# A graph network on one core: GpSimd takes part of the one-hot work in the building of the adjacency matrix, and a small load changes its queue

## The chip, the cores and the metric

The kernel runs as one launch on one core of a Trainium2 chip. The metric is device time in microseconds of that core, as the median of several runs. One further execution was recorded by the hardware profiler; its trace is where every row below comes from. The engines are TensorE (PE, with PEld for its weight loads), VectorE (DVE), ScalarE (ACT), GpSimd (POOL) and SyncE (SP); a q behind a name (ACTq, SPq) marks what the engine's instruction queue does by itself, such as register work and the issuing of DMAs.

## The reference, cut to what matters

Four graph layers follow one another on 3125 nodes and 50000 edges: a three-layer graph convolution, an attention layer, a gated edge layer, and a ten-layer deep graph convolution with norms. The change touches only what comes before the first of them. A graph convolution is

```
deg = segment_sum(w, d)                     # the edges into each node, and its self loop
dinv = where(deg > 0, rsqrt(deg), 0)
norm = dinv[s] * w * dinv[d]
out = segment_sum(h[s] * norm[:, None], d)  # + bias
```

The kernel does the sum over edges as a dense product: it first builds the matrix A of 3125 x 3125 with A[source, target] = sum of the weights w of the edges between them (self loops with weight 1), stores it in DRAM, and the layers read it from there. `dinv` is multiplied in outside of A.

## The kernel before

**What `build_adjacency` does.** The edges come sorted by target. Six target nodes make a group; a group's edges are in `lane_words`, one edge on each of the 128 partitions (122 edges and the 6 self loops), with four words: the row of the source within its tile of 125 nodes, the place of source tile and target, the weight, and the tile. For each group a one-hot of the source row (`ohr`, 128 edges x 125, compared with a ramp) and a weighted one-hot of the place (`cell`, 128 edges x 150) are multiplied on TensorE, which gives the group's six columns of A. Row 125 of the one-hots is all ones, so that the same product gives the degrees.

**Units and blocks.** Three groups make a unit (index `n`, 174 of them), about 25 units make a block of 450 columns (index `b`, seven blocks, `j` is the unit within its block; block 4 has 24 units). For each unit:

- VectorE makes `ohr` (L495, one instruction for the three groups) unless `n % 3 == 1`, and always makes `cell` (L499). Once in four units it makes the factors of the cells (L469, L477, L480).
- ScalarE makes `ohr` for the units with `n % 3 == 1` (`byact`), in four instructions (L587 three times, L590 once), four units ahead (`EARLY`).
- TensorE does the three products (L555; each is recorded as two passes, so a unit has six MATMUL records) into one of five PSUM banks (`BANKS`).
- ScalarE copies the sums from PSUM to the block's columns `stage` (L609).

`ohr` and `cell` are rings of five units (`RING`), so VectorE may be five units ahead of TensorE; five banks let TensorE be five units ahead of ScalarE's copies.

**Extra edges.** A few groups have more than 122 edges. What is left over comes in extra blocks of edges (index `i`; with these inputs eight in all, one for each block of columns and two for block 5). They are handled in loops whose bounds are read from memory by every engine that takes part: SyncE loads the 122 edges' words and the first cell (L631, L632), GpSimd makes their one-hot and cells (L434, L435, L437), TensorE multiplies (L539), ScalarE copies the sum (L598), VectorE adds it to the columns (L453). The extras of block `b - 1` are in TensorE's and ScalarE's program behind unit `j == EXTRA_AT` (2) of block `b`, and in VectorE's behind unit `j == EXTRA_AT + RING` (7). Only when VectorE has added them does SyncE store the block's degree row (L635) and its 5.6 MB of columns (L636).

**Order.** Each engine runs its own program in order; semaphores tie them: `s_oh` counts VectorE's units, `s_ao` ScalarE's one-hots, `s_mm` TensorE's units, `s_ev` ScalarE's copies, `s_om` the words' DMAs (32 for one extra), `s_oo` GpSimd's extras, `s_omm` TensorE's, `s_oc` ScalarE's, `s_od` VectorE's, `s_blk` the finished blocks. After the last block come the degrees, their square root, and the first layer.

## Time and profile before

| | us |
|---|---|
| median of 3 runs (lowest, highest) | 3285.01 (3284.21, 3285.78) |
| the profiled execution's own time | 3285.47 |
| its span, from the first to the last instruction | 3283.5 |
| the stretch from the first product of a unit (L555) to the last extra's addition (L453) | 35.4 to 228.0 |
| TensorE, VectorE, ScalarE, GpSimd busy in the whole span | 3106.7, 1370.8, 1408.2, 846.8 |

The stretch that the change touches is some 6% of the span. Busy time over the whole span says little of it: TensorE's 3106.7 us are mostly the layers behind it. The rows that follow are therefore taken from inside the stretch. "Idle before" in square brackets is how long the engine stood still just before an instruction, and who let it go on.

### The profile page before, as it was taken

The page shows a single profiled execution, that of the slowest core. Times are in us where ns is not written, and L with a number is a line of the kernel's source. Part 1 is how long each engine was busy: PE and PEld are TensorE (multiplying, and loading weights), DVE is VectorE, ACT ScalarE, POOL GpSimd, SP SyncE. Part 2 cuts the span into 40 slices and gives each one's busy share as a digit, 9 for nine tenths or more (in the row PEclk, how much of TensorE's full clock was granted, in tenths as well). Part 3 has the DMA queues.
Part 4 walks back from the last instruction along what each step waited for, and adds up shares of the span by engine and source line. Part 5 has one row for each costly group of instructions (what it writes and reads, how often), then busy time and mean ns, then how long its engine had stood idle before and what let it go on. Part 6 is the DMA issues. An engine that isn't in the chain of part 4 may idle for free. (4 is left out here: it accounts for less than half of the span.)

```text
span 3283.5 us, 45208 instructions
## 1 busy us (share of the span) xinstructions
PE 3106.7 (95%) x14568; PEld 2006.1 (61%) x14568; DVE 1370.8 (42%) x3096; ACT 1408.2 (43%) x2506; POOL 846.8 (26%) x939
## 2 busy tenths in 40 slices
PE   7879999979999998999999799999999999999998
PEld 6865555547788775777777555555555555555554
DVE  7971110125666667999999511111111111111112
ACT  6860000225555555888888423333332222222333
POOL 2010000037777763777777000000000000000000
PEclk8989999989999998999999899999999999999999
DMA  2556667723333323666666467666677766777774
GB/s 90 231 236 243 273 282 286 286 61 83 87 83 83 83 70 92 186 194 184 186 185 183 181 288 288 283 284 281 284 287 290 290 281 281 290 291 298 290 298 169
DMA packets 166699, 709.29 MB, mean 216 GB/s; under 512 B 39287, under 2 KB 133090, under 8 KB 153423
## 3 DMA queue, kind: packets, MB, share of 16 engines
q1 hardware_dynamic: 127865, 618.84, 48.5%
q0 software_dynamic: 33600, 83.09, 9.1%
q10 hardware_dynamic: 5011, 4.48, 0.5%
q8 instruction: 129, 2.11, 0.3%
q14 instruction: 94, 0.77, 0.1%
HBM read 657.91 MB, written 48.07 MB: 215 GB/s over the span
## 5 line engine op out<-in xcount | busy, mean ns | idle before, releaser
L1422 PE MATMUL deep_out_psum<-deep_adjacency,deep_scaled_nodes_odd 125*128 125x450 f32 (+1 forms) x1750 | 669.7, 537 | 0.0
L1422 PE MATMUL deep_out_psum<-deep_adjacency,deep_scaled_nodes 125*128 125x450 f32 (+1 forms) x1750 | 669.7, 537 | 0.0
L1670 POOL DMA_INDIRECT source_rows<-gat_source_rows,pair_src x416 | 396.5, 953 | 575.3 <-POOLq L64 448.8
L1422 PEld LDWEIGHTS deep_out_psum<-deep_adjacency,deep_scaled_nodes_odd 125*128 125x128 f32 x1750 | 328.4, 189 | 299.8 <-issue 298.9
L1422 PEld LDWEIGHTS deep_out_psum<-deep_adjacency,deep_scaled_nodes 125*128 125x128 f32 x1750 | 328.1, 189 | 298.9 <-issue 298.0
L2100 POOL DMA_INDIRECT near_room<-gate_source_rows,pair_src x416 | 395.1, 950 | 141.7 <-issue 119.2
L1480 ACT ACTIVATE deep_squares_high<-deep_aggregate,deep_vectors 128x450 fp32r<-128x450 f32 (+1 forms) x70 | 46.7, 668 | 618.1 <-DVE deep_aggregate L1552 618.1
L1422 PE MATMUL gcn_out_psum<-adjacency_columns,gcn_scaled_nodes 125*128 125x450 f32 (+1 forms) x700 | 268.7, 538 | 0.0
L2198 PE MATMUL gate_banks<-edge_weights,edge_features_t 128*128 128x256 f32 x832 | 248.4, 380 | 0.0
L1566 DVE SCALAR_TENSOR_TENSOR deep_normed<-deep_aggregate,deep_vectors,deep_squares 128x450 f32<-128x450 f32 (+1 forms) x70 | 47.9, 684 | 384.9 <-ACT deep_squares L1489 384.9
L1422 PEld LDWEIGHTS gcn_out_psum<-adjacency_columns,gcn_scaled_nodes 125*128 125x128 f32 x700 | 131.2, 190 | 123.5 <-issue 122.8
L2200 PE MATMUL gate_banks<-gate_target_rows,gate_node_onehot_t 125*128 x1248 | 204.7, 271 | 0.0
L1552 DVE TENSOR_TENSOR deep_aggregate<-deep_out_psum,dinv_all 128x450 f32<-128x450 f32 (+1 forms) x70 | 43.6, 624 | 348.7 <-PE deep_out_psum L1422 348.7
L1487 ACT ACTIVATE deep_squares<-deep_moments,deep_eps 128x450 f32<-128x450 f32 (+1 forms) x70 | 44.4, 634 | 330.0 <-PE deep_moments L1393 330.0
L1824 ACT ACTIVATE score_terms_sloped<-score_terms_psum 128x512 f32<-128x512 f32 x104 | 62.1, 597 | 250.6 <-PE score_terms_psum L1714 245.4
L555 PE MATMUL adjacency_sum<-h_t,dinv_all 128*128 128x150 f32 x1042 | 155.8, 305 | 13.3 <-DVE h_t L499 12.4
L2209 PE MATMUL gate_banks<-gate_node_onehot,gate_messages 128*128 128x125 f32 x832 | 122.0, 290 | 45.6 <-DVE gate_messages L2390 45.6
L1287 POOL TENSOR_TENSOR identity_branch<-identity_branch,x_t 128x450 f32<-128x450 f32 (+1 forms) x7 | 7.9, 1128 | 600.8 <-ACT identity_branch L1271 600.8
L2200 PEld LDWEIGHTS gate_banks<-gate_target_rows,gate_node_onehot_t 125*128 125x128 bf16 x1248 | 120.9, 97 | 66.5
L555 PEld LDWEIGHTS adjacency_sum<-h_t,dinv_all 128*128 128x128 f32 x1042 | 142.7, 196 | 25.8 <-DVE h_t L499 22.3
L1714 PE MATMUL score_terms_psum<-att_node_onehot_t,near_room 125*128 125x128 bf16 x1248 | 155.2, 226 | 0.2
L1712 PE MATMUL score_terms_psum<-ident,source_rows 128*128 128x128 f32 x416 | 119.2, 286 | 33.8 <-issue 23.0
(418 smaller groups left out, 4754.0 us busy)
## 6 DMA issues: line engine op xcount, KB each, us to landing
deep_adjacency<-adjacency SPq DMA_DIRECT2D x69, 5625.0 KB, 16.2
adjacency_columns<-adjacency SPq DMA_DIRECT2D x19, 5625.0 KB, 16.1
adjacency<-adjacency_columns SPq DMA_DIRECT2D x7, 5625.0 KB, 17.7
edge_features<-in_edge_attr_dram SPq DMA_DIRECT2D x416, 64.0 KB
att_node_rows<-pair_dst_rows SPq DMA_DIRECT2D x104, 128.0 KB
gate_node_rows<-pair_dst_rows SPq DMA_DIRECT2D x104, 128.0 KB, 3.3
source_rows<-gat_source_rows,pair_src POOLq DMA_INDIRECT x416, 2.5
near_room<-gate_source_rows,pair_src POOLq DMA_INDIRECT x416
```

The costliest lines, as they stand in the source:

```text
L555: i = nc.tensor.matmul(acc[:, n % BANKS, q * CELLS:(q + 1) * CELLS], ohr[:, n % RING, q, :], cell[:, n % RING, q, :], start=True, stop=True)
L1422: m = nc.tensor.matmul(op[:, n % 2, 0:cols], h[l % 2][:, s, :], ring[0:T, n % 2, s, 0:cols], start=s == 0, stop=s == NS - 1)
L1480: nc.scalar.activation(sq_high[:, 0:cols], yk, ACT.Square, bias=row[0])
L1566: vec.scalar_tensor_tensor(yb[:, 0:cols], yk, vecs[:, l:l + 1], sq[:, 0:cols], ALU.add, ALU.mult).then_inc(s_nm, 1)
L1670: pool.indirect_dma_start(xj[:, b % HOLD, q, :], None, d["h_r"], bass.IndirectOffsetOnAxis(ap=c["pair_src"][:, b * PQ + q:b * PQ + q + 1], ...
L1712: nc.tensor.matmul(o, xj[:, b % HOLD, q, :], c["ident"][:, :], start=True, stop=False, is_transpose=True)
L1714: m = nc.tensor.matmul(o, rows[:, p, bass.ds(tile[q], 1), :].rearrange("r o f -> r (o f)"), oht[:, b % 2, q * 128:(q + 1) * 128], start=Fa ...
L1824: nc.scalar.activation(low[:, b % 2, :], p_z[:, b % 2, :], ACT.Copy, scale=SLOPE).then_inc(s_lo, 1)
L2100: pool.indirect_dma_start(xj[:, b % 4, q, :], None, d["p_src"], bass.IndirectOffsetOnAxis(ap=c["pair_src"][:, b * PQ + q:b * PQ + q + 1], ...
L2198: nc.tensor.matmul(o, e_t[:, b % 2, q * 128:(q + 1) * 128], we[:, :], start=True, stop=False)
L2200: m = nc.tensor.matmul(o, oht[:, b % 2, q * 128:(q + 1) * 128], rows[:, p, bass.ds(tile[q], 1), :].rearrange("r o f -> r (o f)"), start=Fa ...
L2209: m = nc.tensor.matmul(p_a[:, q * T:(q + 1) * T], msg[:, b % 2, q, :], oh[:, b % 4, q, :], start=True, stop=True)
```

## The change

It does four things, all inside `build_adjacency`.

1. GpSimd makes `ohr` for the units of `bypool`: `n % 3 == 0` and `j >= POOL_FROM` (9), in block 0 only up to `n` = 21. That is five units in each block and six in block 3, 36 in all. It takes three instructions of 128 x 125 for a unit (107 in all, since one unit has two groups). VectorE leaves out L495 for them, and TensorE waits for `s_po` as well.
2. GpSimd makes the one-hot and cells of extra `i + 1` in the loop turn of extra `i`, after TensorE has used those of `i`; those of extra 0 are made by code ahead of the loop of block 0.
3. The words of an extra are loaded by ScalarE, on its own DMA queue: those of extra 0 behind unit `n == LISTED_AT` (21), those of extra `i + 1` behind the copy of the sum of extra `i`. SyncE's loop goes away. One more extra than exists is loaded at the end, and ScalarE waits for it.
4. The lower and upper bound that the engines read may be at most `UO - 1`.

```diff
         CHUNK = 4
         SPREAD_AT, PLACED_AT, FIRST_AT, LISTED_AT, DEGREE_AT = 6, 13, 14, 21, 16
         EARLY = 4
+        POOL_FROM = EXTRA_AT + RING + 2
         tab = c["lane_words"]
         ohr = c["dinv_b"][:, 0:RING * SUB * 128].rearrange("p (k q r) -> p k q r", k=RING, q=SUB)
         cell = c["h_t"][:, 0:RING * SUB * CELLS].rearrange("p (k q i) -> p k q i", k=RING, q=SUB)
...
         names = ("onehots_initialised", "onehots_ready", "sums_ready", "sums_read", "extra_loaded", "extra_onehots_ready", "extra_summed", "extra_read",
                  "extra_done", "columns_done", "extra_local", "degrees_copied", "extras_spread", "extras_placed", "extras_listed", "extra_step",
                  "distances_ready", "far_onehots_ready", "sixes_ready", "members_marked", "marks_ready", "degrees_summed", "degree_step", "degree_guarded", "degree_root", "dinv_ready", "dinv_turned",
-                 "dinv_copied")
+                 "dinv_copied", "pool_onehots_ready")
         (s_p, s_oh, s_mm, s_ev, s_om, s_oo, s_omm, s_oc, s_od, s_blk, s_loc, s_dg, s_xs, s_xp, s_xl, s_xv,
-         s_af, s_ao, s_t6, s_mb, s_mk, s_d, s_v, s_in, s_rt, s_n, s_t, s_c) = (c["sems"].take("build_" + n) for n in names)
+         s_af, s_ao, s_t6, s_mb, s_mk, s_d, s_v, s_in, s_rt, s_n, s_t, s_c, s_po) = (c["sems"].take("build_" + n) for n in names)
         s_st = c["adj_stored"]
         units = [(b, j, u) for b in range(NSP) for j, u in enumerate(UNITS[b])]
         ends = [sum(len(UNITS[k]) for k in range(b + 1)) for b in range(NSP)]
         slot = [(b + NSP - HELD) % 2 for b in range(NSP)]
         byact = [n for n in range(len(units)) if n % 3 == 1]
+        bypool = [n for n, (b, j, u) in enumerate(units) if n % 3 == 0 and j >= POOL_FROM and (b > 0 or n < LISTED_AT + 3)]
         block = ctx.enter_context(nc.Block())
 
         def bounds(eng, b):
             if b == 0:
                 eng.wait_ge(s_xl, 1)
-            return [eng.value_load(c["extra_bounds"][0:1, b + k:b + k + 1], min_val=k, max_val=UO) for k in range(2)]
+            return [eng.value_load(c["extra_bounds"][0:1, b + k:b + k + 1], min_val=k, max_val=UO - 1) for k in range(2)]
 
         @block.gpsimd
         def _(pool):
...
             pool.wait_ge(s_p, 2)
             pool.sem_inc(s_oo, 1)
             for b in range(NSP):
+                for n in (n for n in bypool if units[n][0] == b):
+                    u, k = units[n][2], n % RING
+                    g0, m = u[0], len(u)
+                    if n >= RING:
+                        pool.wait_ge(s_mm, n - RING + 1)
+                    for q in range(m):
+                        i = g.tensor_scalar(ohr[:, k, q, 0:T], c["ramp"][:, 0:T], tab[:, 0, g0 + q:g0 + q + 1], None, ALU.is_equal)
+                    i.then_inc(s_po, 1)
+                if b == 0:
+                    pool.wait_ge(s_om, 32)
+                    g.tensor_tensor(local[:, :], more[:, 1:2], first_cell[:, :], ALU.subtract).then_inc(s_loc, 1)
+                    g.tensor_scalar(xohr[:, 0:T], c["ramp"][:, 0:T], more[:, 0:1], None, ALU.is_equal)
+                    pool.wait_ge(s_loc, 1)
+                    g.tensor_scalar(xcell[:, :], c["ramp"][:, 0:CELLS], local[:, 0:1], more[:, 2:3], ALU.is_equal, ALU.mult).then_inc(s_oo, 1)
                 lo, hi = bounds(pool, b)
                 with pool.Fori(lo, hi) as i:
-                    wait_alone(pool, c, s_om, (i + 1) * 32)
-                    wait_alone(pool, c, s_omm, i + 1)
+                    wait_alone(pool, c, s_om, (i + 2) * 32)
+                    wait_alone(pool, c, s_omm, i + 2)
                     g.tensor_tensor(local[:, :], more[:, 1:2], first_cell[:, :], ALU.subtract).then_inc(s_loc, 1)
                     g.tensor_scalar(xohr[:, 0:T], c["ramp"][:, 0:T], more[:, 0:1], None, ALU.is_equal)
-                    wait_alone(pool, c, s_loc, i + 1)
+                    wait_alone(pool, c, s_loc, i + 2)
                     g.tensor_scalar(xcell[:, :], c["ramp"][:, 0:CELLS], local[:, 0:1], more[:, 2:3], ALU.is_equal, ALU.mult).then_inc(s_oo, 1)
 
         @block.vector
...
                     members_of(h + 1)
                 if n % CHUNK == 2:
                     marks_of(h + 1)
-                if n not in byact:
+                if n not in byact and n not in bypool:
                     vec.tensor_tensor(ohr[:, k, 0:m, 0:T], c["ramp"][:, 0:T].unsqueeze(1).to_broadcast([128, m, T]),
                                       tab[:, 0, g0:g0 + m].unsqueeze(2).to_broadcast([128, m, T]), ALU.is_equal)
                 dve.wait_ge(s_mk, h + 1)
...
                 pe.wait_ge(s_oh, n + 1)
                 if n in byact:
                     pe.wait_ge(s_ao, byact.index(n) + 1)
+                if n in bypool:
+                    pe.wait_ge(s_po, bypool.index(n) + 1)
                 if n >= BANKS:
                     pe.wait_ge(s_ev, n - BANKS + 1)
                 for q in range(len(u)):
...
                     wait_alone(act, c, s_omm, i + 2)
                     wait_alone(act, c, s_od, i + 1)
                     nc.scalar.copy(xsum[:, :], xacc[:, 0:CELLS]).then_inc(s_oc, 1)
+                    e0 = act.value_load(c["extra_first"][0:1, bass.ds(i + 1, 1)], min_val=0, max_val=E)
+                    act.dma_start(more[0:EL, :], d["edges"][bass.ds(e0, EL), :]).then_inc(s_om, 16)
+                    act.dma_start(first_cell[:, :], c["extra_cells"][:, bass.ds(i + 1, 1)]).then_inc(s_om, 16)
+                return hi
 
             for n in range(EARLY):
                 if n in byact:
...
                                acc[:, n % BANKS, 0:m * CELLS].rearrange("p (q s j) -> p s q j", q=m, j=G)).then_inc(s_ev, 1)
                 if n + EARLY in byact:
                     onehots(n + EARLY)
+                if n == LISTED_AT:
+                    act.wait_ge(s_p, 2)
+                    act.wait_ge(s_xl, 1)
+                    e0 = act.value_load(c["extra_first"][0:1, 0:1], min_val=0, max_val=E)
+                    act.dma_start(more[0:EL, :], d["edges"][bass.ds(e0, EL), :]).then_inc(s_om, 16)
+                    act.dma_start(first_cell[:, :], c["extra_cells"][:, 0:1]).then_inc(s_om, 16)
                 if b >= 1 and j == EXTRA_AT:
                     extras(b - 1)
-            extras(NSP - 1)
+            extra = extras(NSP - 1)
+            wait_alone(act, c, s_om, (extra + 1) * 32)
             act.wait_ge(s_in, 1)
             nc.scalar.activation(root, safe, ACT.Sqrt).then_inc(s_rt, 1)
             act.wait_ge(s_t, 1)
...
         def _(sp):
             ly.begin(sp, d)
             for b in range(NSP):
-                lo, hi = bounds(sp, b)
-                with sp.Fori(lo, hi) as i:
-                    e0 = sp.value_load(c["extra_first"][0:1, bass.ds(i, 1)], min_val=0, max_val=E)
-                    wait_alone(sp, c, s_oo, i + 1)
-                    sp.dma_start(more[0:EL, :], d["edges"][bass.ds(e0, EL), :]).then_inc(s_om, 16)
-                    sp.dma_start(first_cell[:, :], c["extra_cells"][:, bass.ds(i, 1)]).then_inc(s_om, 16)
                 sp.wait_ge(s_blk, b + 1)
                 first = ORDER[b] * BW
                 sp.dma_start(c["degree_parts"][0:NS, first:first + BW], stage[T:T + 1, slot[b], :, :]).then_inc(s_dg, 16)
```

What stands where, on three engines. Line numbers of the changed kernel differ (before/changed: L609/L631 the copy of a unit's sums, L598/L616 the copy of an extra's, L587 and L590/L605 and L608 ScalarE's one-hots, L416/L418 the bounds, L434, L435, L437/L450, L451, L453 an extra on GpSimd).

ScalarE's queue before, from the one-hots of unit 28 through the extra of block 0 to the next unit's copies:

```order
L587 ACTIVATE dinv_all<-ramp,lane_words 128x125 x3
L590 ACTIVATE dinv_all<-dinv_all 128x3x125
L416 TENSOR_LOAD extra_bounds
L416 ISA x2
L416 TENSOR_LOAD extra_bounds
L416 ISA x2
L595 UNCONDITIONAL_BRANCH
L595 ISA
L31 REGISTER_ALU
L598 COPY extra_sum<-extra_adjacency_sum 128x150
L595 REGISTER_ALU
L595 COMPARE_AND_BRANCH
```

and the same place in the changed kernel, from the extra's copy on:

```order
L616 COPY extra_sum<-extra_adjacency_sum 128x150
L617 ISA
L617 TENSOR_LOAD extra_first
L617 ISA x2
L618 ISA
L618 DMA extra_words<-edge_list 122x4
L619 REGISTER_ALU
L619 DMA extra_first_cell<-extra_cells 128x1
L613 REGISTER_ALU
L613 COMPARE_AND_BRANCH
L631 COPY adjacency_columns<-adjacency_sum 128x25x18 x3
```

A register load, its checks and two DMA issues now stand between the extra's copy and the copies of the following units.

GpSimd's queue in the changed kernel, blocks 0 and 1 (before, only the rows of the loops, with L434, L435 and L437, stand here):

```order
L438 TENSOR_SCALAR dinv_all<-ramp,lane_words 128x125 x15
L442 TENSOR_TENSOR extra_cell<-extra_words,extra_first_cell 128x1
L443 TENSOR_SCALAR extra_source_onehot<-ramp,extra_words 128x125
L445 TENSOR_SCALAR extra_weighted_cell<-ramp,extra_cell,extra_words 128x150
L418 TENSOR_LOAD extra_bounds
L447 ISA
L450 TENSOR_TENSOR extra_cell<-extra_words,extra_first_cell 128x1
L451 TENSOR_SCALAR extra_source_onehot<-ramp,extra_words 128x125
L453 TENSOR_SCALAR extra_weighted_cell<-ramp,extra_cell,extra_words 128x150
L438 TENSOR_SCALAR dinv_all<-ramp,lane_words 128x125 x15
```

The one-hots of block 1 stand behind the loop that makes extra 1, so they wait for that extra's words too. SyncE's queue before, for block 0:

```order
L629 TENSOR_LOAD extra_first
L629 ISA x2
L31 REGISTER_ALU
L631 ISA
L631 DMA extra_words<-edge_list 122x4
L632 REGISTER_ALU
L632 DMA extra_first_cell<-extra_cells 128x1
L635 DMA degree_parts<-adjacency_columns 25x1x450
L636 DMA adjacency<-adjacency_columns 128x11250
```

Of these only the last two stay on SyncE.

## Rows read from the trace of the kernel before

**Rows 1.** The page: its head.
```profile
span 3283.5 us, 45208 instructions
```

**Rows 2.** Windows between ScalarE's copies of extras: busy us (count), clock, DMA.
```profile
core 0: us, PE busy (x) PEld busy (x) DVE busy (x) ACT busy (x) POOL busy (x), PEclk, DMA share, GB/s
...
97.43:123.15 25.72, 22.42 (x156) 20.16 (x155) 24.91 (x61) 22.92 (x58) 2.39 (x3) 1.00 0.56 228
...
151.41:175.94 24.53, 22.74 (x157) 21.14 (x156) 24.11 (x60) 21.99 (x58) 1.64 (x3) 0.96 0.59 238
...
200.79:204.87 4.08, 1.10 (x4) 1.13 (x5) 1.92 (x5) 0.29 (x1) 2.28 (x3) 0.54 0.00 0
```

**Rows 3.** Waits from 69.6 to 226 us: total us, times, longest.
```profile
ACT adjacency_columns L609 <- PE adjacency_sum L555: 11.2, 27, 1.0
...
PE extra_adjacency_sum L539 <- POOL extra_weighted_cell L437: 5.9, 3, 4.0
```

**Rows 4.** Timeline of ScalarE, units 19 to 24 and the first extra: start, duration.
```profile
62.76 1.39 ACT L609 COPY adjacency_columns<-adjacency_sum 128x450 f32<-128x450 f32 x3
...
65.05 0.52 ACT L590 ACTIVATE dinv_all<-dinv_all 128x375 f32<-128x375 f32 x1
65.47 1.39 ACT L609 COPY adjacency_columns<-adjacency_sum 128x450 f32<-128x450 f32 x3
...
72.18 0.28 ACT L598 COPY extra_sum<-extra_adjacency_sum 128x150 f32<-128x150 f32 x1 [1.18 <-issue]
```

**Rows 5.** Timeline, VectorE: a one-hot and the cells behind it.
```profile
62.28 0.53 DVE L495 TENSOR_TENSOR dinv_all<-ramp,lane_words 128x375 f32<-128x375 f32 x1
62.73 0.60 DVE L499 TENSOR_TENSOR h_t<-h_t,group_member_psum 128x450 f32<-128x450 f32 x1
```

**Rows 6.** SyncE's load of one extra's words: the register load, the issues, GpSimd's start.
```profile
L629 SPq TENSOR_LOAD <-extra_first x8: 282/978/1169, 62.9 to 209.5; - x8
...
63.75 0.30 SPq L631 DMA_DIRECT2D extra_words<-edge_list  x1
64.16 0.59 SPq L632 DMA_DIRECT2D extra_first_cell<-extra_cells  x1
...
66.20 0.83 POOL L434 TENSOR_TENSOR extra_cell<-extra_words,extra_first_cell 128x1 f32<-128x1 f32 x1 [32.29 <-DMA extra_first_cell<-extra_cells]
```

**Rows 7.** GpSimd's instructions, alone and beside VectorE's.
```profile
L435 POOL TENSOR_SCALAR extra_source_onehot<-ramp,extra_words x8: 610/615/1091, 67.0 to 224.8; 128x125 f32<-128x125 f32 x8
...
67.64 1.61 POOL L437 TENSOR_SCALAR extra_weighted_cell<-ramp,extra_cell,extra_words 128x150 f32<-128x150 f32 x1
67.97 0.22 DVE L469 TENSOR_TENSOR group_member_psum<-ramp,lane_words 128x72 f32<-128x72 f32 x1
68.12 0.53 DVE L495 TENSOR_TENSOR dinv_all<-ramp,lane_words 128x375 f32<-128x375 f32 x1
...
146.01 0.88 POOL L437 TENSOR_SCALAR extra_weighted_cell<-ramp,extra_cell,extra_words 128x150 f32<-128x150 f32 x1
146.16 0.71 DVE L495 TENSOR_TENSOR dinv_all<-ramp,lane_words 128x375 f32<-128x375 f32 x1
```

**Rows 8.** Timeline at the first and second extra on TensorE, and GpSimd's last.
```profile
69.65 0.49 PE L539 MATMUL extra_adjacency_sum<-extra_weighted_cell,extra_source_onehot 128*128 128x150 f32 x2 [1.05 <-POOL extra_weighted_cell L437]
70.05 4.07 PE L555 MATMUL adjacency_sum<-h_t,dinv_all 128*128 128x150 f32 x30
...
201.10 0.19 POOL L434 TENSOR_TENSOR extra_cell<-extra_words,extra_first_cell 128x1 f32<-128x1 f32 x1 [2.57 <-DMA extra_first_cell<-extra_cells]
203.77 0.84 PE L539 MATMUL extra_adjacency_sum<-extra_weighted_cell,extra_source_onehot 128*128 128x150 f32 x2 [3.96 <-POOL extra_weighted_cell L437]
...
224.63 0.19 POOL L434 TENSOR_TENSOR extra_cell<-extra_words,extra_first_cell 128x1 f32<-128x1 f32 x1 [21.25 <-DMA extra_first_cell<-extra_cells]
...
227.41 0.28 ACT L598 COPY extra_sum<-extra_adjacency_sum 128x150 f32<-128x150 f32 x1 [1.80 <-PE extra_adjacency_sum L539]
```

**Rows 9.** A window of 2 us behind TensorE's 4 us stop (columns as in Rows 2).
```profile
204.00:206.00 2.00, 2.00 (x9) 2.00 (x10) 0.32 (x1) 0.28 (x1) 0.00 (x0) 0.50 0.00 0
```

## The prediction

> **What bounds the kernel now.** The span is 3283.5 us [rows 1], and the profiled execution took 3285.47 us, 0.46 above the median; what moves inside the span moves the time one for one, because TensorE goes straight on into the first layer when the stretch is over. I read the windows between ScalarE's copies of two extras first, since in order of program one such copy stands in each block and 25 units lie between two of them. In [rows 2] the 25.72 us window has VectorE busy for 24.91: it is the bound there. But ScalarE has 22.92, and in the 24.53 us window it is hardly behind. Then I looked for how fast ScalarE could go at all. In [rows 4] it works without a pause: the copies of units 19 to 21 start at 62.76, those of 22 to 24 at 65.47, so three units with one set of one-hots take 2.71 us, 0.90 a unit, 22.6 for 25. To this comes the reading of the bounds ahead of an extra (idle 1.18 at 72.18 [rows 4]) and the extra's copy; part of the reading can lie beside the engine's last instruction, so I take 1.0 for both. ScalarE alone would need 23.6 us for a block. VectorE needs for three units two one-hots, three cells and three quarters of the factors: its slot for a one-hot is 0.45 us (62.28 to 62.73 [rows 5]). TensorE does five units in 4.07 us [rows 8], 0.81 a unit, and is not the bound. So VectorE bounds most blocks, with ScalarE 2 us behind it. From 69.6 to 226 us ScalarE waited 11.2 us for TensorE's sums [rows 3]; that is all the room the change can open before ScalarE is the bound.
>
> **One-hots to GpSimd.** 36 one-hots leave VectorE: 36 x 0.45 = 16.2 us. Two or three of block 0 (n = 9, 12, 15) fall where VectorE waits for TensorE's ten extra products anyway. Were VectorE the only limit, about 15 us would go. It is not: the room is 11.2 us.
>
> GpSimd's price for one: three instructions like L435, at 0.61 us [rows 7], 1.8 us; its units come every three, some 2.7 us apart, so it keeps up if nothing holds it. What could hold it shows in [rows 7]: the cells of an extra took 0.88 us in one place and 1.61 in another, where VectorE's L469 (0.22) and L495 (0.53) ran at the same time; the difference, 0.73, is their sum. At 146.16 it was VectorE that was held: 0.71 for an instruction of 0.53. The Trainium skill (SBUF — State Buffer, "Who interferes with whom") says that a VectorE instruction with two SBUF inputs contends with a GpSimd instruction that reads SBUF, and that one of them blocks. L495 and L469 read two SBUF tensors, and the trace agrees by the 0.73. I take 1.8 to 2.9 us a unit: the high end is 1.8 and all of VectorE's such instructions in three units, one L495 (0.53) and three quarters of the factors (about 0.5). The 4 units of lead that the ring gives, 3.3 us or more, cover either.
>
> **The words on ScalarE's queue.** This is the cost. On SyncE the register load begins at 62.9, the first issue at 63.75, and the second ends at 64.16 + 0.59 = 64.75: 1.85 us [rows 6]. On ScalarE this train stands behind the extra's copy, and the next copy, which came 0.2 us after the extra's, cannot be dispatched before it is through: 1.75 us more for each. The cheapest reading is the two issues alone, 0.30 + 0.50 = 0.8; the dearest has the register load at SyncE's median of 0.98 and a blocked issue, near 3. I take 1.75, since nothing else is on this queue and the store of the block comes after. Seven such trains lie ahead of the last extra's copy, 12.25 us; the one behind unit 21 begins while L590 (65.05) still runs and holds the copies from 65.47, 1.4 us, at a place where ScalarE has no room [rows 4]. Sum 13.65 us. The train behind the last copy, and ScalarE's wait for it, lie beside the last degree row's way to TensorE through VectorE and SyncE, and cost nothing; without that cover they would cost 1.85.
> The Trainium skill (DMA: Bandwidth & Descriptors, "Issuing engines are not separate DMA queues") holds that all queues run on the same 16 DMA engines and another issuer saves only sequencer time. By that rule the move gives the transfer nothing and only shifts the 1.85 us from an idle engine to a busy one.
>
> **Extras one block early.** Before, the words of the last extra came at 224.63, and ScalarE's last extra copy waited 1.80 us; it would have been through the bounds 1.1 us sooner than 227.41 [rows 8]. That 1.1 is won. TensorE's other waits for GpSimd (5.9 us in three [rows 3]) are mostly the second extra of block 5, which does not get better. Now its words are issued only behind the first one's copy: 1.85 for the train, 1.45 until GpSimd starts (64.75 to 66.20 [rows 6]), 2.67 until TensorE starts (201.10 to 203.77) and 1.10 until ScalarE's copy, 7.1 us in place of 4.08 [rows 2, 8]. That is 3.0 longer, of which 1.75 is counted: 1.25 more.
>
> **What is late next.** GpSimd makes extra i + 1 before the one-hots of its block. From TensorE's product of an extra (0) ScalarE's copy comes at about 2.5 (69.65 to 72.18), the train ends at 4.4, GpSimd starts at 5.8, is through at 8 and has its first unit at 10.2. TensorE wants unit j = 9 at about 8.2 (the one-hots of j = 7 come from ScalarE at 6.4, behind the train, then 0.9 a unit). So it is 2 us late in blocks 3 and 6, whose first unit is j = 9, one in blocks 2 and 5 (j = 10), nothing in 1 and 4 (j = 11). ScalarE has two copies in hand then and loses about half: 2.1 us in all, taken from its room.
>
> **Sum.** + 13.65 (trains) + 1.25 (second extra) + 2.1 (late first units) - 11.2 (ScalarE's waits for sums) - 1.1 (last words) = + 4.7 us. 3285.0 + 4.7 = 3289.7 us. A measurement of this kernel tells some 0.2% (6.6 us) from no change, so I expect none that counts: 0.50 for within 6.6 us by this mechanism.
>
> **Rivals.**
> *ScalarE's train is cheap, and VectorE's relief shows* (0.20, faster). If the train costs the two issues alone, 0.8 each, and partly lies where ScalarE waits, the trains come to 6.4 less some 3 and the sum is - 5 to - 8; at no price at all it is VectorE's 15 us less 2 for the rest, 3272. I put 3277. For it: in the 25.72 us window ScalarE had 2.8 us free. Against: the 24.53 us window is within 0.9 of ScalarE's own need. It decides at a train under 0.9 us.
> *GpSimd is the bound* (0.20, slower). If each reading instruction is fully blocked by VectorE's, a unit takes 2.9 us where the cycle is 2.7, and what starts 2 us late stays late to the block's end. Six blocks at 2 to 3 us: + 15, less nothing, since ScalarE is the bound behind it; with the sum of the other terms 3285 + 2.6 + 12 = 3300. For it: the 1.61 us [rows 7]. Against: most L435 ran in 0.61 beside a busy VectorE. It decides at 2.7 us a unit.
> *TensorE's clock* (0.10, slower). Behind its stop of 3.96 us it was granted 0.50 of full speed, the 1.2 GHz level, and did 9 matmuls in 2 us [rows 8, 9]. If every block's new stop did that, each would cost 1 to 1.5 us of the slack: + 7, with the sum 3296.
>
> **Range and chances.** The bounds of the train move the sum by 8 x 0.95 down and 8 x 1.2 up, GpSimd's by 12 up. 8 in 10 lies in 3277 to 3301; the likeliest case alone in 3284 to 3296. Faster by more than 6.6 us 0.18, within 0.50, slower 0.32: the forecast's own upper edge adds to the slower rivals.
>
> **What the changed trace would show.** ScalarE: behind each extra's copy 1.7 to 1.9 us without work, its waits for sums under 3 us. VectorE: idle for 10 us or more that it had not been. GpSimd: units at 1.8 to 2.3 us. TensorE: waits for GpSimd's one-hots in blocks 3 and 6, hardly in 1 and 4; the second extra of block 5 some 7 us behind the first. The last sum of a unit no earlier than 225. I am wrong if ScalarE still waits 8 us or more for sums, or if its gap behind an extra is under 1 us.

## The result, and the profile after

| | before | changed |
|---|---|---|
| median of 4 runs each (lowest, highest), us | 3285.40 (3284.21, 3286.71) | 3309.68 (3308.34, 3310.02) |
| span of the profiled execution, us | 3283.5 | 3308.0 |
| from the first product of a unit to the last extra's addition, us | 35.4 to 228.0 = 192.6 | 36.6 to 253.5 = 216.9 |

The ratio is 1.0073, with a 95% interval from 1.0061 to 1.0085: slower by 24.3 us. The forecast was 3289.7 with a range of 3277 to 3301; the result is 20.0 above the one and 8.7 above the upper edge of the other. The stretch alone is longer by 216.9 - 192.6 = 24.3 us, so the whole loss lies in it. From here on "the stretch" is this length.

The windows between ScalarE's copies of extras, after, in the last four blocks (columns as in [rows 2]):

```profile
125.20:153.16 27.96, 24.28 (x179) 22.88 (x178) 24.26 (x58) 23.90 (x63) 13.60 (x21) 1.00 0.51 209
153.16:179.31 26.15, 22.48 (x154) 21.43 (x153) 22.54 (x54) 22.03 (x57) 10.60 (x17) 0.93 0.55 224
179.31:214.45 35.14, 23.51 (x134) 21.65 (x132) 23.80 (x56) 22.80 (x58) 10.53 (x18) 0.76 0.41 166
214.45:220.89 6.44, 1.11 (x4) 1.14 (x5) 0.32 (x1) 0.28 (x1) 1.64 (x3) 0.63 0.02 0
220.89:252.93 32.04, 21.07 (x139) 20.14 (x138) 15.41 (x36) 18.64 (x47) 10.45 (x18) 0.81 0.44 182
```

The first is as long as its block before (28.3), the second 1.6 us longer (24.5 before). The third and the fifth are some 10 us too long, every engine is idle for some 11 us or more in them, and the granted clock fell to 0.76 and 0.81. The fourth is the second extra of block 5, 6.44 in place of the 4.08 of [rows 2]. So the loss is not a tax on each block; two places hold most of it. The waits from 69.6 to 252 us (columns as in [rows 3]):

```profile
POOL extra_cell L450 <- DMA extra_first_cell<-extra_cells: 88.6, 7, 20.5
ACT adjacency_columns L631 <- PE adjacency_sum L573: 28.9, 16, 9.9
...
PE adjacency_sum L573 <- issue: 18.1, 10, 9.7
...
POOL dinv_all L438 <- PE adjacency_sum L573: 17.0, 19, 1.8
...
PE extra_adjacency_sum L555 <- POOL extra_weighted_cell L453: 6.6, 1, 6.6
```

ScalarE now waits 28.9 us for sums where it waited 11.2 [rows 3], the longest 9.9 and not 1.0. TensorE's own longest wait is 9.7 us, "issue": the profile names no releaser. The timeline of all engines there, in block 5 (start, duration, idle before in brackets; SyncE's and ScalarE's DMA issues are the rows with SPq and ACTq), says who it was:

```profile
180.10 0.48 ACTq L618 DMA_DIRECT2D extra_words<-edge_list  x1
180.68 0.51 ACTq L619 DMA_DIRECT2D extra_first_cell<-extra_cells  x1
181.24 0.45 SPq L659 DMA_DIRECT2D adjacency<-adjacency_columns  x1
...
187.65 0.54 ACT L631 COPY adjacency_columns<-adjacency_sum 128x450 f32<-128x450 f32 x1 [0.34 <-PE adjacency_sum L573]
...
190.48 0.19 POOL L450 TENSOR_TENSOR extra_cell<-extra_words,extra_first_cell 128x1 f32<-128x1 f32 x1 [20.46 <-DMA extra_first_cell<-extra_cells]
...
192.09 3.49 POOL L438 TENSOR_SCALAR dinv_all<-ramp,lane_words 128x125 f32<-128x125 f32 x6
193.96 1.34 PE L573 MATMUL adjacency_sum<-h_t,dinv_all 128*128 128x150 f32 x4 [6.34 <-issue]
```

The words of the next extra are issued, done at 181.19; 0.05 us later SyncE begins to issue the block's store (called 5.6 MB above; it is 128 rows of 11250 numbers, 45 KB each, 5.76 MB in all). GpSimd can start on the words only at 190.48, 9.3 us after their issue, against the 1.45 of [rows 6]. GpSimd's first one-hots of the block (L438) stand behind the loop that waits for those words, so they come at 192.09, and TensorE starts again at 193.96, 1.87 us later, when three of these six instructions (3.49 / 2 = 1.75 us) are through. The DMA view shows what the words met (queue, kind: packets, MB, share of the 16 engines' time; q1 carries SyncE's DMAs, q10 ScalarE's). In block 5, from 180 to 184 us, from 184 to 190, and of that from 186 to 190:

```profile
q1 hardware_dynamic: 34, 0.58, 45.9%
q10 hardware_dynamic: 232, 0.00, 3.0%
...
q1 hardware_dynamic: 71, 2.84, 111.4%
q10 hardware_dynamic: 36, 0.00, 0.3%
...
q10 hardware_dynamic: 7, 0.00, 0.1%
```

The two loads are 268 small packets of 16 or 4 bytes. In block 4 all 268 were on their way by 155.95 us, before the first packet of q1. In block 5 only 232 were by 184; the other 36 come one by one or a few together between the store's packets, seven of them behind 186, and none behind 190. From 184 to 190 q1 has 63 packets of 45 KB, which took some 1.7 us each (111.4% of 16 engines and 6 us, over 63). So the late packets of the words wait for turns of the store that last 1.7 us each, and the last of them for several.

### The profile page after: what moved, and what is told of

Same layout as the page of the kernel before. It is cut to its first block and busy times, and to the rows that moved or that the text cites. A ratio compares the mean times of both kernels' runs of the same rounds, so it can differ in the third digit from the quotient of the medians.

```text
span 3308.0 us, 45234 instructions
## 1 busy us (share of the span) xinstructions
PE 3110.3 (94%) x14568; PEld 2016.7 (61%) x14568; DVE 1355.1 (41%) x3060; ACT 1407.6 (43%) x2507; POOL 917.1 (28%) x1049
## 5 line engine op out<-in xcount | busy, mean ns | idle before, releaser
L573 PE MATMUL adjacency_sum<-h_t,dinv_all 128*128 128x150 f32 x1042 | 156.7, 310 | 34.9 <-issue 18.4
L1575 DVE TENSOR_TENSOR deep_aggregate<-deep_out_psum,dinv_all 128x450 f32<-128x450 f32 (+1 forms) x70 | 43.6, 623 | 348.7 <-PE deep_out_psum L1445 348.7
L573 PEld LDWEIGHTS adjacency_sum<-h_t,dinv_all 128*128 128x128 f32 x1042 | 148.6, 204 | 42.3 <-issue 21.9
## 6 DMA issues: line engine op xcount, KB each, us to landing
deep_adjacency<-adjacency SPq DMA_DIRECT2D x69, 5625.0 KB, 16.2
adjacency_columns<-adjacency SPq DMA_DIRECT2D x19, 5625.0 KB, 16.2
adjacency<-adjacency_columns SPq DMA_DIRECT2D x7, 5625.0 KB, 17.7
```

The source lines that it names most:

```text
L573: i = nc.tensor.matmul(acc[:, n % BANKS, q * CELLS:(q + 1) * CELLS], ohr[:, n % RING, q, :], cell[:, n % RING, q, :], start=True, stop=True)
```

## The race, block by block

Issue of the words' second DMA (start plus duration), the store's issue, and GpSimd's start, in the changed kernel; the last column is the time from the words' issue to GpSimd's start on them:

| block | words' issue ends | store's issue starts, ends | GpSimd starts | words' issue to GpSimd |
|---|---|---|---|---|
| 1 | 76.96 | 77.19, 78.66 | 79.04 | 2.08 |
| 2 | 102.53 | 102.62, 103.31 | 103.97 | 1.44 |
| 3 | 127.05 | 127.90, 128.35 | 128.50 | 1.45 |
| 4 | 155.02 | 155.10, 155.79 | 156.46 | 1.44 |
| 5 | 181.19 | 181.24, 181.69 | 190.48 | 9.29 |
| 6 | 222.92 | 222.82, 223.27 | 233.62 | 10.70 |

Where the store's issue ends 0.77 us or more behind the words' the load takes 1.4 to 2.1 us; where it ends 0.50 or 0.35 behind, 9 to 11. The words have to be through before SyncE's packets come: in block 4 they were, in block 5 they were not, as the DMA view shows. Block 6's is the second stop:

```profile
237.10 7.01 PE L573 MATMUL adjacency_sum<-h_t,dinv_all 128*128 128x150 f32 x42 [9.75 <-issue]
```

The Trainium skill (DMA: Bandwidth & Descriptors, "Queues, rings and completion order") says that a DMA engine serves its queues in turn and changes only between packets. By that rule a small load on another queue should be late beside a large store, yet not by the whole of it. The trace agrees: the words' packets went on between the store's, seven of them behind 186 us, and were through after some 9 us, where the store took 17.3 us from its issue to its landing. How the packets were spread over the 16 engines the trace does not tell.

## The experiments

The chips of these runs granted TensorE less clock in later stages of the network (kernel before: medians of 3805.89 for e1 to e4, 3712.97 for e5 to e8, 3708.51 for e9 and e10), and the totals scatter by more than the effects. From 600 to 1200 us of the span, for one, the clock was 0.96 before and 0.78 in e9. In the stretch and up to 600 us it was 1.00 but for low spans of 3 to 20 us behind pauses of TensorE, so the stretch is what I compare. Three kernels ran twice, and their stretches differed by 1.8, 1.3 and 0.2 us; before's 192.6 is from one profile. Starts and ends are rounded to 0.1 us, and so is what is said below.

The time from one ScalarE copy of an extra to the next (first column: first product of a unit to the first such copy), made of the starts of those instructions in each trace:

| kernel | to the first | b1 | b2 | b3 | b4 | b5 | second extra | b6 | stretch |
|---|---|---|---|---|---|---|---|---|---|
| before | 36.8 | 25.3 | 25.7 | 28.3 | 24.5 | 24.9 | 4.1 | 22.5 | 192.6 |
| changed | 38.5 | 25.6 | 24.5 | 28.0 | 26.2 | 35.1 | 6.4 | 32.0 | 216.9 |
| e10 changed again | 38.3 | 25.6 | 24.5 | 30.0 | 25.7 | 34.3 | 6.4 | 33.3 | 218.7 |
| e1 store waits | 37.6 | 25.6 | 25.5 | 28.0 | 25.7 | 27.5 | 6.4 | 23.6 | 200.6 |
| e2 no GpSimd one-hots | 38.4 | 26.4 | 25.5 | 27.8 | 25.3 | 26.3 | 6.4 | 21.9 | 198.4 |
| e3 one-hots alone | 37.2 | 23.8 | 24.7 | 25.6 | 23.2 | 24.1 | 4.0 | 22.5 | 185.7 |
| e4 words by SyncE | 36.7 | 23.8 | 24.1 | 25.4 | 23.2 | 23.4 | 4.5 | 22.2 | 183.9 |
| e8 e4 again | 35.9 | 23.8 | 24.1 | 25.4 | 23.2 | 23.4 | 4.5 | 21.6 | 182.6 |
| e7 e4 with idle trains | 36.6 | 25.5 | 25.4 | 27.3 | 26.9 | 27.1 | 4.4 | 21.9 | 195.7 |
| e6 words a turn early | 37.1 | 23.7 | 24.1 | 25.1 | 23.3 | 23.5 | 2.5 | 21.5 | 181.6 |
| e9 e6 again | 35.9 | 23.7 | 24.1 | 25.1 | 23.3 | 23.5 | 2.8 | 22.3 | 181.4 |
| e5 words behind the store | 35.9 | 43.2 | 42.0 | 46.5 | 42.3 | 43.6 | 5.4 | 39.4 | 298.8 |

### e1: SyncE's store waits for the words

```diff
             for b in range(NSP):
+                lo, hi = bounds(sp, b)
                 sp.wait_ge(s_blk, b + 1)
...
+                wait_alone(sp, c, s_om, (hi + 1) * 32)
                 sp.dma_start(d["adj"][ORDER[b]], stage[:, slot[b], :, :]).then_inc(s_st[slot[b]], 16)
```

> The changed kernel, with one wait more: SyncE issues a block's 5.6 MB store only when the words of the next extra have landed. Theory A (the words lose a race with the store on the DMA engines, and GpSimd's one-hots are queued behind the words): the stops of TensorE of 6.3 and 9.8 us in blocks 5 and 6 go, with 3 us of low clock behind them; 3288 to 3294 us, words landing 1.5 to 2.5 us behind their issue in every block. Theory B (GpSimd's one-hots are slowed by VectorE's reads and bound the blocks): nothing changes, 3303 to 3312. Theory C (ScalarE's issue trains are the loss): 3303 to 3312 as well, since the trains stay.

The stretch was 34.4 to 235.0 = 200.6 us; total 3821.35 against 3805.89, ratio 1.0041 (1.0012 to 1.0070). In block 5 the store went a microsecond after the words, not at the same time:

```profile
178.20 0.51 ACTq L619 DMA_DIRECT2D extra_first_cell<-extra_cells  x1
...
179.97 0.33 SPq L661 DMA_DIRECT2D adjacency<-adjacency_columns  x1
...
180.16 0.19 POOL L450 TENSOR_TENSOR extra_cell<-extra_words,extra_first_cell 128x1 f32<-128x1 f32 x1 [12.64 <-DMA extra_first_cell<-extra_cells]
```

The words took 1.45 us again (in block 6 3.05, where only the block's degree row, 25 packets of 1.8 KB, was in their way). Both long stops are gone, and with them 216.9 - 200.6 = 16.3 of the 24.3 us: block 5 is shorter by 7.6 and block 6 by 8.4. Only the order of two transfers was changed: that is the race. 8.0 us stay.

### e2: no one-hots on GpSimd

```diff
-        bypool = [n for n, (b, j, u) in enumerate(units) if n % 3 == 0 and j >= POOL_FROM and (b > 0 or n < LISTED_AT + 3)]
+        bypool = []
```

> The changed kernel with an empty list of GpSimd's units: VectorE makes those one-hots again; the early extras and the words on ScalarE's queue stay. Theory A: late words hold nobody but the extra itself, which is needed 20 us later, so no stop of TensorE over 2 us but the second extra of block 5; VectorE bounds again and the trains take ScalarE's room: 3286 to 3297. Theory B: the same, so this run does not tell A from B. Theory C: 3300 or more, since the trains stay.

34.9 to 233.3 = 198.4 us; ratio 1.0023 (0.9989 to 1.0058). ScalarE's trains are all there, and the race is lost in the same two blocks: in block 5 the words' issue ends at 180.08 and GpSimd starts at 189.35, 9.3 us later; in block 6 it is 10.8. But no unit stands behind the words, and no stop before a unit's product is over 2.0 us. So the late words hurt by way of GpSimd's one-hots. Against e1 the one-hots are worth + 2.2 us, hardly more than the 1.8 by which two profiles of one kernel differed: with the trains on ScalarE, no gain of VectorE's relief is to be seen.

### e3: GpSimd's one-hots alone

The kernel before with the `bypool` lines of the diff for GpSimd, VectorE and TensorE, and nothing else.

> The kernel before with the 36 units' one-hots on GpSimd and nothing else of the change: SyncE loads the words, and an extra's one-hots are made in its own block, behind that block's unit one-hots. Theory A: no unit waits for words of the same moment; ScalarE becomes the bound without any train, 4 to 10 us faster than before, 3275 to 3282. Theory B: GpSimd's pace bounds here too, slower than before, 3295 or more. Theory C: 3275 to 3282.

36.0 to 221.7 = 185.7 us, - 6.9; ratio 1.0016 (0.9980 to 1.0053). The waits from 34 to 260 us:

```profile
POOL dinv_all L438 <- PE adjacency_sum L567: 63.1, 35, 8.7
...
ACT adjacency_columns L621 <- PE adjacency_sum L567: 15.4, 21, 3.1
PE extra_adjacency_sum L549 <- POOL extra_weighted_cell L447: 13.9, 8, 3.7
```

GpSimd waited 63.1 us for rings to come free: it was early, not the bound. What this version pays is TensorE's 13.9 us of waits for extras (7.5 before, in the same window), since GpSimd reaches them behind its own units.

### e4 and e8: the words by SyncE, ahead of the store

ScalarE's loads go away, and SyncE gets a loop in place of them:

```diff
+                lo, hi = bounds(sp, b)
+                with sp.Fori(lo, hi) as i:
+                    e0 = sp.value_load(c["extra_first"][0:1, bass.ds(i + 1, 1)], min_val=0, max_val=E)
+                    wait_alone(sp, c, s_omm, i + 2)
+                    sp.dma_start(more[0:EL, :], d["edges"][bass.ds(e0, EL), :]).then_inc(s_om, 16)
+                    sp.dma_start(first_cell[:, :], c["extra_cells"][:, bass.ds(i + 1, 1)]).then_inc(s_om, 16)
                 sp.wait_ge(s_blk, b + 1)
```

> The changed kernel, but SyncE issues the words of extra i + 1, as soon as TensorE has used extra i and ahead of the block's store in its own queue; ScalarE issues nothing in the loops. Theory A: no race and no trains, the words land before the store starts: 3276 to 3287. Theory B: 3300 or more. Theory C: 3276 to 3290, the time of the trains (12 us) off the one of e1_store_waits or more. e1_store_waits less this run is the price of the trains: 12 us if ScalarE is the bound all the way, 3 to 8 if it has room.

35.2 to 219.1 = 183.9 us, - 8.7; the interval of the total's ratio, 1.0005 to 1.0145, is wide and its centre (1.0075) on the other side of the medians (3797.43 against 3805.89), so the total says nothing. The same kernel once more, e8:

> The same kernel as e4_words_by_sync, beside the other three on one chip: stretch 183 to 185, and a time that can be set against theirs; where the chip grants TensorE its clock as it did for the changed kernel, 3274 to 3280 us.

34.5 to 217.1 = 182.6 us, - 10.0; ratio 0.9988 (0.9939 to 1.0038). The stretch is 0.4 under what I had expected. The first and second part of the change shorten the stretch when ScalarE's queue has no part in them: from e1 to e4 it is 16.7 us.

### e7: e4, and the trains on ScalarE with nothing behind them

```diff
                     nc.scalar.copy(xsum[:, :], xacc[:, 0:CELLS]).then_inc(s_oc, 1)
+                    e0 = act.value_load(c["extra_first"][0:1, bass.ds(i + 1, 1)], min_val=0, max_val=E)
+                    wait_alone(act, c, s_id, i * 32 + 1)
+                    act.dma_start(idle_words[0:EL, :], d["edges"][bass.ds(e0, EL), :]).then_inc(s_id, 16)
+                    act.dma_start(idle_cell[:, :], c["extra_cells"][:, bass.ds(i + 1, 1)]).then_inc(s_id, 16)
```

> e4_words_by_sync with ScalarE's trains put back without a use: behind each extra's copy ScalarE loads the register and issues the same two DMAs, into tiles that nobody reads; the real words still come by SyncE ahead of the store. Only the price of the trains is added. Theory A with my 1.75 us for each: 8 x 1.75 less what ScalarE had as room, stretch 183.9 + 5 to 14 = 189 to 198. Theory C (the trains are the whole loss of the change): 210 or more.

35.4 to 231.1 = 195.7 us: 11.8 over e4, 13.1 over e8; ratio 1.0014 (0.9970 to 1.0059). Block by block over e4 (from the unrounded starts): 1.66, 1.36, 1.89, 3.69, 3.66, then - 0.07 and - 0.26. Blocks 4 and 5 pay double. TensorE in e7, block 4:

```profile
153.09 1.84 PE L575 MATMUL adjacency_sum<-h_t,dinv_all 128*128 128x150 f32 x6 [2.15 <-ACT adjacency_columns L635]
```

and the windows around it, first e7, then e4 at the same place of the program (columns as in [rows 2]):

```profile
152.00:154.00 2.00, 0.92 (x4) 0.95 (x5) 2.00 (x7) 1.60 (x5) 1.12 (x2) 0.76 0.90 286
154.00:156.00 2.00, 1.59 (x7) 1.26 (x7) 2.00 (x6) 1.97 (x7) 0.00 (x0) 0.50 0.92 345
156.00:158.00 2.00, 2.00 (x10) 2.00 (x10) 1.78 (x5) 1.97 (x7) 0.73 (x1) 0.50 0.84 360
158.00:160.00 2.00, 2.00 (x10) 2.00 (x10) 0.98 (x2) 0.91 (x2) 1.29 (x3) 0.53 0.89 383
```

```profile
149.00:151.00 2.00, 1.45 (x11) 1.22 (x10) 2.00 (x5) 1.97 (x7) 1.46 (x3) 1.00 0.93 346
151.00:153.00 2.00, 2.00 (x18) 2.00 (x17) 2.00 (x7) 1.98 (x6) 0.63 (x2) 1.00 0.84 360
```

While ScalarE issues, no copy frees a bank; TensorE stops for 2.15 us, and behind the stop it is granted 0.50, the 1.2 GHz level, for some 7 us: 10 matmuls in 2 us in place of 18. Then ScalarE, in the 158 window busy for 0.91 us, waits for it. Block 5 has the same: a stop of 2.45 us, and 0.50 for 6.8 us behind it. Each of the two costs about 2 us more than a train. The stop alone does not do it. Blocks 2 and 3 have stops of 2.41 and 2.23 us and pay 1.36 and 1.89; behind the first the clock was at 0.50 for 3.4 us, behind the second it stayed at 1.00:

```profile
102.00:104.00 2.00, 1.84 (x7) 1.88 (x8) 1.80 (x5) 2.00 (x7) 1.74 (x3) 0.50 1.16 476
...
128.00:130.00 2.00, 1.83 (x14) 1.63 (x14) 2.00 (x6) 1.97 (x6) 1.80 (x4) 1.00 1.02 410
```

What is paid twice is thus a span of some 7 us at the low level. e10 below has such a span in a kernel that was not edited at all.

### e5: the words behind the store

The words of the next block's extra are issued by SyncE directly after the store, so that all races are lost.

> Words by SyncE as in e4_words_by_sync, but the words of the next block's extra are issued behind this block's store, so that the race is lost in each of the six blocks 1 to 6 (the column numbers of the eight extras are written out for these inputs; ScalarE issues nothing). The measure is the stretch from the first product of a unit to the last extra's addition, which the trace gives whatever the rest of the chip does: 192.6 us before, 216.9 changed, 200.6, 198.4, 185.7 and 183.9 in the four runs so far. Theory A (race and queue): six stops of TensorE of 6 to 10 us, words landing 9 us or more behind their issue; stretch 235 to 260. Theory B (GpSimd's pace) and C (ScalarE's trains): as e4_words_by_sync, 182 to 190.

33.8 to 332.6 = 298.8 us, ratio 1.0304 (1.0213 to 1.0396). TensorE stopped for 17.2, 18.7, 19.8, 17.6, 17.6 and 16.2 us, once in each block from 1 to 6, twice as long as I had expected. The first of them:

```profile
71.85 0.44 SPq L661 DMA_DIRECT2D adjacency<-adjacency_columns  x1
...
73.74 2.60 SPq L653 DMA_DIRECT2D extra_first_cell<-extra_cells  x1
89.59 0.19 POOL L450 TENSOR_TENSOR extra_cell<-extra_words,extra_first_cell 128x1 f32<-128x1 f32 x1 [24.57 <-DMA extra_first_cell<-extra_cells]
...
93.07 1.34 PE L573 MATMUL adjacency_sum<-h_t,dinv_all 128*128 128x150 f32 x4 [17.23 <-issue]
```

On the store's own queue GpSimd starts on the words 17.7 us after the store's issue (89.59 - 71.85), when the store is over. The direction held and the size not. Two things differ here from the change, the queue and that the words are issued behind the store and not just ahead of it; which of them makes the whole store out of 9 to 11 us, no run separates.

### e6 and e9: the words one turn early

SyncE issues the words of extra i + 1 as soon as GpSimd has used those of i (`wait_alone(sp, c, s_oo, i + 2)` in e4's loop), not when TensorE has used its one-hots.

> As e4_words_by_sync, but SyncE issues the words of extra i + 1 as soon as GpSimd has made extra i, nearly a block ahead of their use, instead of when TensorE has used extra i. Theory A: words are never waited for, even where they lie behind a store; the second extra of block 5 comes 4 us behind the first in place of 5 or more; no stop of TensorE over 3 us behind the first products; stretch 178 to 184. Theory B: 195 or more. Theory C: as e4_words_by_sync, 182 to 186.

35.9 to 217.5 = 181.6 us, - 11.0; the second extra comes 2.5 us behind the first, where I had expected 4; total 3708.65 against 3712.97, ratio 0.9978 (0.9936 to 1.0021). Once more, in five rounds, e9:

> The kernel with the words loaded by SyncE one turn early, once more and in five rounds, to see what the total time says of it. Race theory (what holds GpSimd's one-hots up is a load of words that stands in the DMA engines behind or beside the block's store; what the trains cost is ScalarE's own time): with neither race nor trains, the stretch from the first product of a unit to the last extra's addition is again 181 to 184 us against 192.6 of the kernel before, so the time is 9 to 12 us under the kernel before, a ratio near 0.997. Rival (the store, coming later, costs in the first layer what the building saved): the stretch is 181 to 184, but the time is within 3 us of the kernel before.

33.8 to 215.2 = 181.4 us, - 11.2; total 3701.82 against 3708.51, ratio 0.9989 (0.9952 to 1.0026). The two stretches agree within 0.2 us. The total leans the same way, but the interval spans 1: the single runs of before beside e9 go from 3699 to 3747 us, and 11 us can't be told from none. Between the gain of the stretch and the rival of e9 (given back later) this leaves the answer open.

### e10: the changed kernel again

No edit.

> The changed kernel once more, with no edit, for how firmly the race falls. If which blocks lose it is fixed by the order of the instructions, the stretch is again 215 to 219 us, with two stops of TensorE of more than 6 us before a unit's product, in blocks 5 and 6. If the words go by a gap of a few hundred ns that varies from one execution to another, the number of such stops is another one (one to four), and the stretch goes by 8 us for each. The time is 20 to 28 us over the kernel before in the first case.

36.4 to 255.1 = 218.7 us; total 3729.45 against 3708.51, ratio 1.0056 (1.0037 to 1.0075), some 21 us. The long stops are the same two:

```profile
195.20 6.45 PE L573 MATMUL adjacency_sum<-h_t,dinv_all 128*128 128x150 f32 x36 [6.33 <-issue]
237.55 8.21 PE L573 MATMUL adjacency_sum<-h_t,dinv_all 128*128 128x150 f32 x42 [8.76 <-issue]
```

The words' issue ends and the store's starts at 182.45 and 182.50 in block 5, 156.73 and 156.81 in block 4: the same 0.05 and 0.08 us as in the first trace, one lost and one won. What differs is the issue of the store, which took 0.44 us in the one and 0.69 in the other. In both traces, and in e2, the same two blocks lose and no other; so in these three the race falls by the order of the program, not by chance.

Where the two traces of this kernel part is block 3, 28.0 us in the first and 30.0 here. The stop before it is the same, 2.01 and 2.00 us, but not the clock behind it (first the first trace, then this one):

```profile
129.27 1.77 PE L573 MATMUL adjacency_sum<-h_t,dinv_all 128*128 128x150 f32 x12 [2.01 <-DVE h_t L515]
132.00:134.00 2.00, 1.63 (x13) 1.66 (x14) 0.83 (x3) 1.33 (x4) 2.00 (x4) 1.00 1.36 585
...
128.92 2.08 PE L573 MATMUL adjacency_sum<-h_t,dinv_all 128*128 128x150 f32 x12 [2.00 <-DVE h_t L515]
132.00:134.00 2.00, 1.96 (x8) 1.99 (x9) 0.08 (x1) 0.47 (x2) 1.67 (x3) 0.50 0.89 382
```

It was at 0.50 for 6.8 us here and not at all in the first trace, and the block is 2.1 us longer. That is what one such span comes with when nothing is edited, and it is the size of the 2 us of blocks 4 and 5 of e7.

## Why the prediction was wrong

**The step that failed** is in "What is late next": "the train ends at 4.4, GpSimd starts at 5.8". It gives every load of words the 1.4 us that one took [rows 6], at a place with no store in flight. In blocks 5 and 6 the load took 9.3 and 10.7 us, and TensorE stopped for 6.3 and 9.8 us where the list of late units had 1 and 2. That is 16.3 us (e1) on a term of 2.1, more than the 11.3 from the forecast to the range's upper end; the rest of the sum alone would have ended inside the range, at 3293. The premise stands at the train's price, "since nothing else is on this queue and the store of the block comes after". The queue was empty, but the 16 DMA engines behind it were not. The store comes after by 0.05 to 0.85 us in blocks 1 to 5 and in block 6 begins 0.10 us before the words' issue ends; I took it as a cover without asking by how much. The trace of before had the numbers. Its store in block 5,

```profile
178.04 0.42 SPq L636 DMA_DIRECT2D adjacency<-adjacency_columns  x1
```

is issued 2.10 us after the start of the extra's copy (175.94 [rows 2]), and a train of 1.75 us behind a copy of 0.28 ends at 2.03: a tie. The price of the train itself was right in the sum.

**The chain behind it** I had half: "GpSimd makes extra i + 1 before the one-hots of its block" was right. That one late transfer thereby holds GpSimd, TensorE and ScalarE up, I did not follow; e2 shows it, where words as late harm nobody. The list of late blocks is off too: block 4 has 24 units, so it is block 5 whose first unit of GpSimd is j = 11 and block 6 where it is j = 10; the 2.1 us fit this list (half of 2.0 + 1.1 + 1.1) and not the one in words.

**The rest of the sum.** Without the race it is + 4.7 forecast and + 8.0 measured (e1). The last two rows are put down to their terms by their place alone; no run takes either away by itself:

| term | forecast | measured | from |
|---|---|---|---|
| relief and last words | - 11.2 - 1.1 = - 12.3 | - 8.7, - 10.0 | e4, e8 |
| trains behind extras | 12.25 | 11.8, 13.1 | e7 less e4, e8 |
| train behind unit 21 | 1.4 | 1.0 | first column, e1 less e7 |
| second extra, beyond its train | 1.25 | 2.0 | its column, e1 less e7 |
| late first units | 2.1 | 1.7 | b6, e1 less e7 |

With e4 for the first two these are - 8.7 + 11.8 + 1.0 + 2.0 + 1.7 = 7.8; the rest is rounding and the other columns, in which e1 and e7 differ by up to 1.2 us either way. In block 6 of e1 the words were 1.6 us late by the degree row, so its 1.7 are not all of the kind forecast. What was mis-sized is the relief: I took all of ScalarE's waits for sums as room, but from 34 to 260 us they fell only from 20.2 to 14.1 (e4), and the last block gave little: 22.5 us before, 22.2 in e4, 21.6 in e8. The trains' sum is right by luck, for its parts are not: 1.4 to 1.9 in blocks 1 to 3, 3.7 in blocks 4 and 5, nothing behind them. ScalarE's gap is as forecast (copy of an extra at 179.31, the next copy at 181.35, idle 1.75 before it). The second extra came 6.4 us behind the first, 7.1 forecast. The one-hots with trains present cost 2.2 us (e1 against e2) where the forecast had 2.1 and no gain; with profiles of one kernel 1.8 apart, that agreement proves little.

**The rivals.** "GpSimd is the bound" came nearest to the time (3300, with 3309.7 measured) for a wrong reason: the median of its 107 instructions was 605 ns, so 1.8 us for the three of a unit, and it waited for TensorE for 17.0 us of 69.6 to 252 us. "TensorE's clock", at 0.10, was right for blocks 4 and 5 of e7 and block 3 of e10, with 2 us each, and not for every block. "The train is cheap" fell with e7. Of the signs that I had named, "ScalarE's waits for sums under 3 us" failed (28.9), and so I am wrong by the bound of 8 us that I had set. So it would have without the race: e1 has 22.7 from 34 to 260 us, where before has 20.2. ScalarE had its trains and its waits too: in blocks 4 and 5 of e7 its pause made TensorE stop, and behind the stop ScalarE waited for a slow TensorE.

**The clock** does not explain the races. In the window of block 5's stop,

```profile
188.00:190.00 2.00, 0.00 (x0) 0.00 (x0) 0.28 (x1) 0.19 (x1) 0.00 (x0) 0.50 0.89 383
```

nothing computes, the DMA engines are busy for 0.89 with the store, and TensorE comes back at the 1.2 GHz level. It had been there since 182, behind a stop of 2.30 us at ScalarE's train; e1 has the same stop and the same 0.50 behind it, and not the 6.34 us.

## What to carry to other kernels

When a load moves to another queue, look not at what stands on that queue but at what the same DMA engines will be carrying when it is issued, and write the distance to the next large transfer in microseconds beside it; an order that holds by a tenth of a microsecond is a race, and a wait of the large transfer for the small one took 16.3 us off here (e1). Ask then what else stands behind the instruction that waits for the small load: work put on an engine ahead of a deadline of its own inherits every wait of the queue before it. And a DMA issue on an engine without room can cost its time twice, where it makes TensorE stop and a span of low clock follows, as in two of the five blocks of e7 in which the train cost anything.

## What the runs showed of the hardware

- Two loads of 122 and 128 partitions (2 KB and 0.5 KB) took 1.44 to 2.1 us from the end of the issue to GpSimd's start, 9.3 and 10.7 us on another queue beside a 5.76 MB store whose issue ended 0.50 and 0.35 us later, and on the store's own queue, behind it, 15.9 us from the start of the second issue (which itself took 2.60), 17.7 from the store's. In e1, where no store is in flight, they took 1.44 to 2.2 us, and 3.05 in block 6 beside the 44 KB of a degree row.
- The step between is sharp: with the store's issue ending 0.77 us behind the words' they were not held, with 0.50 they were, in both traces of the changed kernel and in e2.
- The held packets of the small load went on between the store's packets of 45 KB, some 1.7 us each: of 268, 36 were left at 184 us, seven at 186, none at 190.
- How long TensorE had stopped did not by itself decide whether the clock fell. In e7 stops of 2.15 and 2.45 us were followed by 0.50 for 6.8 us each (so was the 4 us stop of [rows 8]), one of 2.41 by 3.4 us, one of 2.23 by none; in the changed kernel a stop of 2.0 us was followed by 6.8 us in one execution and by none in the other. A pause of 1.00 us in block 4 of e4 left the clock at 1.00.
